# TensorE waits for its own semaphore counts in the attention stage of a graph network kernel

## The reference, cut to what matters

```python
s = einsum('nhc,nhc->nh', Qh, Kh) / sqrt(32)              # one score per node and head, 8 heads
alpha = leaky_relu(s[src] + s[dst], 0.2)                  # per edge, self loops included
m = segment_max(alpha, dst); e = exp(alpha - m[dst])
a = e / segment_sum(e, dst)[dst]
attn = segment_sum(Vh[src] * a[:, :, None], dst)          # N x 256
h = batch_norm(x + attn @ Wo + bo)                        # then a feed-forward layer, batch norm
```

## The kernel before

| step | line | what it makes | count, and who waits for it |
|---|---|---|---|
| turn_tops | L1270 | last column of the first scan, transposed | tops_turned: VectorE L995 |
| turn_carries | L1274 | the partition scan, turned back | carry_ready: VectorE L1001 |
| sums(before, 2) | L1249 | third quarter of the sums of the block before | quarters_used: GpSimd |
| select_maxima | L1280 | 17 small bf16 products, the selected maxima | max_selected: VectorE L1019 |
| sums(before, 3) | L1249 | fourth quarter, five columns | quarters_used: GpSimd, VectorE L1069 |
| prepare(after, chunks 0 and 1) | L1257, L1264 | bias and eight one-hot columns, transposed | bias_turned, T_ready: ScalarE L1172, L1175 |
| spread_nodes | L1290 | 17 small bf16 products in two halves | first_spread, last_spread: VectorE L1038, twice |
| prepare(after, the rest) | L1264 | nine more one-hot columns | T_ready: ScalarE L1175 |
| turn_attended(before) | L1297 | attended rows, transposed | att_turned: ScalarE L1203 |
| sums(this, 0) | L1249 | first quarter of this block's sums | quarters_used: GpSimd |
| project(before) | L1305 | product with Wo | projected: VectorE L1086 |
| sums(this, 1) | L1249 | second quarter | quarters_used: GpSimd |

## Time and profile before

### The profile page before, as it was taken

How to read it: one execution, slowest core, us unless ns; L and a number is a source line. 1 busy time by engine, 2 the same in 40 slices (tenths; PEclk the granted TensorE clock), 3 DMA queues, 4 the chain that set the end, 5 groups by cost and what they waited for, 6 DMA issues and landing times. The chain is left out here.

```text
span 4893.1 us, 71187 instructions
## 1 busy us (share of the span) xinstructions
PE 3799.9 (78%) x15901; PEld 2488.7 (51%) x15902; DVE 2235.7 (46%) x7891; ACT 1434.7 (29%) x2745; POOL 2679.8 (55%) x4185
## 2 busy tenths in 40 slices
PE   3886645656566556986999999688888888779999
PEld 1233324444444444875677777344444444457777
DVE  6997756767676677345121121222222222222222
ACT  3983222222222222245344444100000000023333
POOL 6781056676766666013544444266666666646664
PEclk9999977777777777985999999799998999889999
DMA  4442233333333333026767666477777776646665
GB/s 138 176 184 92 58 82 92 95 97 96 96 96 96 94 96 86 0 67 179 201 183 206 189 183 185 138 211 210 214 210 206 209 214 206 197 135 208 204 202 178
DMA packets 346846, 734.87 MB, mean 150 GB/s; under 512 B 77407, under 2 KB 171229, under 8 KB 341985
## 3 DMA queue, kind: packets, MB, share of 16 engines
q0 software_dynamic: 176144, 461.72, 33.4%
q10 hardware_dynamic: 100178, 157.63, 10.3%
q1 hardware_dynamic: 70268, 113.00, 6.7%
HBM read 622.28 MB, written 109.84 MB: 150 GB/s over the span
## 5 line engine op out<-in xcount | busy, mean ns | idle before, releaser
L900 POOL DMA_INDIRECT a_gathered<-table,record x850 | 808.2, 951 | 642.6 <-issue 378.5
L2258 POOL DMA_INDIRECT l_gathered<-table,record x782 | 761.0, 973 | 472.1 <-issue 283.4
L2451 PE MATMUL bank<-l_gathered,l_onehot 128*125 128x512 f32 x1564 | 777.0, 652 | 179.1 <-DMA l_gathered<-table,record 110.7
L1828 POOL DMA_INDIRECT l_gathered<-table,record x578 | 546.1, 945 | 463.4 <-PE bank L2036 215.9
L1249 PE MATMUL bank<-a_gathered,a_onehot 128*125 128x264 f32 x1700 | 570.3, 494 | 101.6 <-DVE a_gathered L1053 79.0
L2451 PEld LDWEIGHTS bank<-l_gathered,l_onehot 128*125 128x125 f32 x1564 | 316.3, 207 | 617.3 <-issue 457.6
L1942 ACT ACTIVATE l_part<-l_packed 128x1000 fp32r<-128x1000 bf16 (+1 forms) x396 | 413.3, 1070 | 554.4 <-PE bank L2017 227.1
L1249 PEld LDWEIGHTS bank<-a_gathered,a_onehot 128*125 128x125 f32 x1700 | 393.5, 243 | 203.9 <-issue 76.5
L2017 PE MATMUL bank<-rows_first,l_part 125*125 125x512 f32 x1650 | 406.6, 405 | 29.3 <-ACT l_part L1942 29.2
L2017 PE MATMUL bank<-rows_last,l_part 125*125 125x512 f32 x1650 | 394.5, 398 | 11.3 <-ACT l_part L1942 9.9
L2017 PEld LDWEIGHTS bank<-rows_first,l_part 125*125 125x125 f32 x1650 | 308.4, 187 | 121.2 <-issue 43.9
(11 more groups left out here) (282 smaller groups left out, 5515.3 us busy)
## 6 DMA issues: line engine op xcount, KB each, us to landing
l_packed<-adjacency ACTq DMA_DIRECT2D x265, 250.0 KB
adjacency<-d_stage SPq DMA_DIRECT2D x35, 1562.5 KB
l_packed<-adjacency ACTq DMA_DIRECT2D x132, 281.2 KB
l_gathered<-table,record POOLq DMA_INDIRECT x1360
a_gathered<-table,record POOLq DMA_INDIRECT x850
table<-rows_first POOLq DMA_DIRECT2D x50, 250.0 KB, 3.5
table<-l_work ACTq DMA_DIRECT2D x50, 250.0 KB
l_source_rows<-table ACTq DMA_DIRECT2D x50, 250.0 KB
```

The lines of the kernel that those rows point to most:

```text
L900: pool.indirect_dma_start(out=gathered0[s][:, j * TW:(j + 1) * TW], out_offset=None, in_=table0, in_offset=bass.IndirectOffsetOnAxis(ap=re ...
L1828: pool.indirect_dma_start(out=gathered[g][:, j, :], out_offset=None, in_=table, in_offset=bass.IndirectOffsetOnAxis(ap=record[k.t][:, j, 0 ...
L2258: pool.indirect_dma_start(out=gathered[:, j * w:(j + 1) * w], out_offset=None, in_=table, in_offset=bass.IndirectOffsetOnAxis(ap=record[t] ...
L2451: last = pe.matmul(total[0:NB, 0:w], onehot[t][:, j, :], rows[:, j, :], start=False, stop=(j == T - 1), skip_group_check=True)
```

## The change

TensorE gets a wait for the count that it has just given, behind turn_tops, turn_carries, select_maxima, each half of spread_nodes, and behind sums of the quarters 0, 2 and 3. Nothing is put behind quarter 1, prepare, turn_attended and project. No computation, buffer or order changes, and no other engine's stream.

```diff
@@ sums(s, i, q)
                     last.then_inc(quarters_used[s], 1)
+                    if q != 1:
+                        pe.wait_ge(quarters_used[s], r * NQ + q + 1)
@@ turn_tops, turn_carries
                     pe.transpose(mix_ps[s][0:HEADS, 0:P], local[s][:, :, T - 1], identity[:, :]).then_inc(tops_turned[s], 1)
+                    pe.wait_ge(tops_turned[s], r)
...
                     pe.transpose(node_ps[1][:, CARRY:CARRY + HEADS], scanned[s][:, 0:P], identity[0:HEADS, 0:HEADS]).then_inc(carry_ready[s], 1)
+                    pe.wait_ge(carry_ready[s], r)
@@ select_maxima
                     last.then_inc(max_selected[s], 1)
+                    pe.wait_ge(max_selected[s], r)
@@ spread_nodes, in the loop over the two halves
                         last.then_inc(spread[s], 1)
+                        pe.wait_ge(spread[s], r)
```

## The result

The changed kernel takes 5,045.0 us (median of 5 runs, 5,021.7 to 5,048.7) against 4,995.4 us (median of 5, 4,991.9 to 5,006.5): ratio 1.009, 95% interval 1.007 to 1.0111. I had forecast 4,972 us, faster. The time lies inside the range of 4,932 to 5,048 and 2 us from the price of the rival "PE is held by the late counts" (5,043), on the other side of no change than my forecast.

What follows compares the result with a forecast made beforehand. It took a ring of POOL's gather, DVE and TensorE's sums, with late TensorE counts, as the bound. Gain -33 us plus 10 us of uncovered waits gave -23 us: 4,995.4 to 4,972 us, with an 8-in-10 range of 4,932 to 5,048.

Steps and rivals of the forecast that it cites:

- PE is held by the late counts: Attention: quarter 3 and one-hot chunks wait for late counts, 1 us per block, 5,043 us; slower had 0.30, mostly this.
- What bounds the kernel: Attention stage: no engine full; gather, buffers and sums form a ring; a faster TensorE side could return about 65.7 us.
- The tops: Wait behind the tops: PE loses nothing, since its next instruction already waits for DVE's L995, which needs this count.
- Uncovered overlap: Other seven waits: lost load and matmul overlap, 0.31 to 0.44 us each, mostly hidden; 0.2 us per block left, 10 us.
- A wait brings late counts sooner: TensorE's counts in attention: draining PE after bursts makes late counts prompter, recovering half of POOL's 65.7 us wait, 33 us.
- Nothing measurable: Attention: lateness from outside TensorE's stream with waits hidden, or gains lost to DVE's row wait; 0 to 10 us; chance 0.26.

Runs made afterwards that it cites:

- the control: The kernel before, run again unedited on chip 13 with its own trace: 4,955.4 us against 4,960.0, ratio 0.9991.
- the doubled burst: Kernel before plus the wait behind the selected maxima, their 17 products made twice: 4,933.9 us, ratio 1.0086 on chip 7; ratio 1.0 on chip 0, 0.9996 on chip 3.
- the drained burst: Kernel before plus only the wait behind the selected maxima: 4,977.0 us, ratio 1.0037 on chip 13; 1.0013 on chip 7; 0.9997 on chip 3.

## Why the prediction was wrong

**What bounds the kernel** was right as far as it went: a ring between POOL's gather, DVE and PE's sums, and counts of TensorE seen 2 to 4 us after the modelled ends. It missed that this was the state of the chip that made the trace. On chips 0, 3 and 14 the same program shows no late count and is 5% faster than on chip 13.

**The tops: nothing.** The one run with the waits behind tops and carries gives 1.0, but on chip 0, where no wait costs. Not shown for late counts.

**Uncovered overlap: 10 us.** The mechanism is there at the size I gave it. The 0.31 us was from start to start, 0.386 + 0.14 - 0.22, with 0.14 us for the restart; the idle time behind a drain measures 0.15 to 0.16 us, and that is the restart. The whole weight load that would have made it 0.44 isn't in it. For all eight waits together the time moved by 4.5 us by the medians (interval -1 to +8) on chip 3. Near enough, and not the reason.

**A wait brings late counts sooner: -33 us.** This is the step that failed. I took half of 65.7 us because "the late counts follow the densest bursts that PE issues" and "a wait empties PE after each burst". The runs showed: the count that PE waits for comes no sooner. With PE drained behind the burst it still took 3.4 us (block at 1348.30), the stall behind the maxima is 2.4 us in the mean on chip 13 and 2.08 on chip 7, and a burst twice as long left it at 2.13. With the whole change DVE's idle ahead of L995, L1019 and L1038 was no smaller in sum than in the control (116.5 to 114.5 us). On chip 7 later counts did gain, 17 us of DVE's idle (43.3 against 60.6 for the three), and the time still rose by 20 us. That is because the sum had no term for the other side: it put what PE loses while a count is held back at nothing and left it to a rival. In the place of -33 us stand quarter 3's late start and its slower matmuls, with DVE's 40 to 59 us of idle before L1069, and the stalls behind the spread. The shape that I read as cause (bursts are followed by lateness) was only where the rows let lateness be seen. The counter-example that I had in hand, the tops with nothing behind them and a count 3.65 us late, was the better evidence, and I gave it half the weight.

**The rival "PE is held"**, at 5,043 us, was the case. The hold is one of counts and not of matmuls, as the bunch at 1305.09 to 1305.25 shows. The rival's mechanism: quarter 3 behind the maxima, then the one-hot columns behind the spread. PE's stalls in those places are 80.2 us, 46.8 us and 38.4 us in the changed kernel's trace. Its price, 1 us per block, measured 50 us / 50 blocks. Its sum has no term for quarter 3 at half the clock, which the changed kernel pays on top. That the hit is so close is partly luck: the price is 0.58% on chip 7 and within noise on chips 0, 3 and 14, and I had taken "a third of 2.85 us" by feel. I wrote that it decides "from the point where the counts behind waits come more than about 1.5 us late"; the mean stall behind the maxima was 2.4 us on chip 13 (17 us slower) and 2.08 us on chip 7 (8 us slower), and 0.15 us cost nothing, which is in keeping with that point.

**Nothing measurable** is what happens on chips with prompt counts, and the second half of this rival's reason holds there: DVE waits for the gathered rows and PE's stalls are slack. Its first half, late counts with the waits hidden, isn't what those chips show, since no count is late on them.

On the Trainium skill: "Perfetto Trace Analysis", Tensor Engine Instruction, has matmul ends as the profiler's estimates. By that rule alone a wait could only cost, and the direction agrees. But misjudged ends aren't the cause here: ten matmuls can't have run in the 0.13 us between the two counts at 1305.09 and 1305.22. On chip 3 the next matmul starts 0.15 us after the modelled end.

**What stays open.** Why TensorE's counts are late on some chips. Not the burst's own work (the doubled burst), not what is issued behind it (the drained burst). The granted clock of the stage is 0.75 in the traces of the control and the changed kernel and 0.78 with prompt counts; whether it has a part in it wasn't tried. The lateness is almost wholly TensorE's: of the counts whose time the trace keeps between 690 and 1,900 us, 323 of 616 of PE's are over 0.1 us late in the control, against 7 of 1,209 of DVE's and none of 336 of ACT's and 514 of POOL's; on chip 0 (tops and carries) none of any engine is. It isn't all that sets the chips apart: of the 259 us between the spans of these two traces, 88 have gathered by the attention's last sum and 171 come behind it. No run changed anything outside TensorE's stream, so a cause there was neither tried nor excluded.

## What to carry to other kernels

An engine should wait for its own count only where it needs the result: the wait doesn't bring that count sooner, and it makes the engine a second hostage of whatever delays the count. If such a wait must stand, put work between it and the instruction that gives the count: one step later, 91.5 us of stall became 15, though the 14 us of time that this saved are at the edge of the noise. A clock that is the same in the mean can still fall on other matmuls: look at it under the instructions that the change moves. Before a small change is judged by a trace, look at whether "remote" and odd releasers in the waits mean late counts on that chip, and repeat on another. (The traces of chips 7 and 13 also keep only about half as many count updates, 32,518 in the control against 68,097 in that of tops and carries on chip 0. So an "issue" there can be a wait whose update is missing.) Repeating pays: the price of the same eight waits was 50 us, 20 us and nothing that could be measured.

## What the runs showed of the hardware

- The same program took 4,696 to 4,698 us on three chips, 4,884 on one and 4,960 on another, at a mean granted clock of 0.903, 0.890 and 0.885. The clock alone wasn't tried as a cause.
- On the last two TensorE's counts reach other engines, and TensorE itself, up to several us after the modelled end of the matmul, and in bunches: those of the maxima and of quarter 3 come 0.13 us apart where the work between them is over 2 us. On the first three they are there within 0.2 us. VectorE's, ScalarE's and GpSimd's counts are prompt on all five, but for 5 to 12 of VectorE's some 1,200 in the traces with late counts. The lateness behind the maxima falls into two classes of about equal number: on chip 7, 23 stalls of 3.2 us in the mean (73.6 / 23) and 21 of 0.85 us (17.9 / 21).
- A wait of TensorE for its own prompt count leaves it idle for 0.15 us.
- Behind 17 and behind 34 small products the mean stall for the late count was the same, 2.08 and 2.13 us.
- Where counts are late, a wait in front of quarter 3's matmuls put more of them at half the clock: 24 of 450 took over 0.6 us without it, 161 of 440 with it, on chip 13.
